# Local attention with in-place exponentials, PSUM operands, a new slot order and f16 three-product projections

## The chip, the cores and the metric

The program runs on one core of one Trainium2 chip. The metric is the device time of one execution in microseconds; the number quoted for a version is the median of several executions.

## What is computed

The input is 8 sequences of 512 tokens with 128 features. First comes a clustered attention with its own MLP, then two layers of rotary local attention, each followed by a gated FFN. The change touches only the local attention of the two layers:

```python
h = shift_token(x)
qkv = h @ wqkv                       # 128 -> 3*512
q = l2norm(q) * qs ; k = l2norm(k) * ksc
q, k = rotary_xpos(q, k)             # q*cos*scale + rotate_half(q)*sin*scale
sim = jnp.einsum('bhwid,bhwjd->bhwij', bq, bk)      # 8 heads of 64, window 64, own + previous window
attn = jax.nn.softmax(sim, axis=-1)                 # banded mask
out = jnp.einsum('bhwij,bhwjd->bhwid', attn, bv)
x = x + o @ wo
h = shift_token(x)                   # and its mean and variance, for the FFN
```

## The kernel before, in words

`local_attention` is called once per layer. The 8 x 512 tokens make 32 tiles of 128 tokens, four tiles to a sequence. Each of the five engines runs its own hand-written list of steps, one `slot(n)` per tile; semaphores alone tie the engines together. A tile passes through five slots: in slot n TensorE (PE) projects tile T = n to q, k and v; N = n-1 gets its norms; R = n-2 is transposed; U = n-3 gets scores, maxima and exponentials; O = n-4 gets its division by the row sums, the transposition of the probabilities and the product with v. At the end of a sequence, three more steps follow, a slot apart: the product with `wo` and the addition to x (slots with n mod 4 = 0), the token shift and its mean (0 and 1), the squares and their mean (1 and 2).

The steps that the change touches, with their lines before:

- PE: `project` (L1313) writes f32 products into a ring of two PSUM banks, used in turn with `transpose` (L1325) of the rotated q and k. `ring_free` says whose reader must be done before a bank is written again. `scores` (L1336 the mask, L1343 the products) writes `s_ps`, two PSUM banks. `prob_turn` (L1355) transposes the probabilities, `weigh` (L1369) multiplies them with v, L1399 is the product with `wo`.
- ScalarE (ACT): `take_raw` (L1556) copies q and k from the ring to SBUF as `raw`; `squares` (L1600); `take_qT` (L1563), `take_values` (L1579), `take_out` (L1571) copy from PSUM; `exps` (L1544) reads `s_ps`, writes `prob` in SBUF, head by head, with the row sum as accumulator; `inverse_norms` (L1588, L1591); `shift_tokens` (L1538, L1539) makes `hT`.
- VectorE (DVE): `share` (L1475, L1477) divides `prob` in SBUF by the sums; `maxima` is a reduction over `s_ps` (L1461) and a tiny product of two SBUF operands, the exponentials' bias (L1467); `rotate` (L1442) multiplies the swapped halves of `raw` by the sines, both operands in SBUF; `take_probT` (L1495) and `take_kT` (L1488) copy from PSUM; `norms` (L1451, and L1455 the clip).
- GpSimd (POOL): `polish` (L1644 to L1650, four tiny steps), `scale_keys` (L1670), `shift` (L1681, L1683), `spin` (L1657 the cosine product, L1663 the sum with `swapped`).

## Time and profile before

| | |
|---|---|
| runs shown | 1634.2, 1635.84, 1637.27 us; median 1635.84 |
| profiled execution | 1636.19 us, of which the span from first to last instruction is 1634.4 |
| busy over the whole span | PE 80%, DVE 78%, ACT 61%, POOL 53% |
| local attention, layer 0 and 1 | 358.2 and 360.6 us |
| gated FFN, layer 0 and 1 | 79.5 and 80.1 us |
| mean granted TensorE clock | 0.925 of full speed |

Busy time is the union of an engine's instructions. Times in the trace are microseconds from the start of the span. An f32 matmul of 512 columns stands as two instructions in the trace, an f16 one as one. An instruction's duration is a little longer than the distance to the next one's start, as the engines overlap the end of one with the start of the next.

### The profile page before, as it was taken

Reading aid. Unit: us, or ns where it says so; the run is one execution under the profiler, and the core shown is the slowest. Engines: PE = TensorE matmul, PEld = TensorE weight load, DVE = VectorE, ACT = ScalarE, POOL = GpSimd, SP = SyncE. Lnnn points to the kernel's source line nnn. Section 1 sums busy time; section 2 is a strip of 40 time slices with the busy share of each in tenths; the row PEclk is TensorE's granted clock in tenths of the full one; section 3 lists DMA queues with packets and bytes.
Section 4 is the critical chain, followed back from the end, with each engine's and each line's share of the span. In section 5 each row is a group of like instructions: output and inputs, shape, how many; then the busy total and the mean of one; then the engine's idle time right before and its main releaser. Section 6 shows DMA issues by size and latency. Waiting matters only on the chain. (4 is left out here: it accounts for less than half of the span.)

```text
span 1634.4 us, 26635 instructions
## 1 busy us (share of the span) xinstructions
PE 1314.9 (80%) x9094; PEld 619.7 (38%) x9156; DVE 1267.1 (78%) x1905; ACT 989.5 (61%) x2252; POOL 871.0 (53%) x989
## 2 busy tenths in 40 slices
PE   3488998989989875776788888868778888888596
PEld 1122222222222213453455555543335555555343
DVE  5778888878888634336999999959569999999593
ACT  4246666666666662225788887743257777777522
POOL 4566767676766001114777777730067777777100
PEclk8579999999999997787999999998979999999898
DMA  3433333333333101001111111101011111111001
GB/s 102 93 59 65 66 65 66 65 65 62 69 59 70 23 1 51 1 2 33 24 24 24 24 24 24 24 7 40 12 24 24 24 24 24 24 24 24 1 0 54
DMA packets 161402, 60.92 MB, mean 37 GB/s; under 512 B 139722, under 2 KB 153076, under 8 KB 161268
## 3 DMA queue, kind: packets, MB, share of 16 engines
q1 hardware_dynamic: 161268, 59.22, 17.1%
q8 instruction: 74, 1.21, 0.3%
q14 instruction: 60, 0.49, 0.1%
HBM read 8.73 MB, written 2.10 MB: 7 GB/s over the span
## 5 line engine op out<-in xcount | busy, mean ns | idle before, releaser
L639 DVE TENSOR_REDUCE row_max<-max_ps 128x2 f32<-128x1024 f32 x256 | 313.0, 1223 | 70.3 <-PE max_ps L451 68.9
L691 ACT ACTIVATE prob<-scores_ps 128x1024 f32<-128x1024 f32 x256 | 262.2, 1024 | 147.5 <-PE scores_ps L431 144.0
L1313 PE MATMUL la_ring<-lw_wqkv,la_hT 128*128 128x512 f32 x384 | 230.4, 687 | 26.5 <-ACT la_hT L1539 13.6
L1544 ACT ACTIVATE la_prob<-la_s,la_bias,la_inv 128x128 f32<-128x128 f32 x512 | 229.1, 474 | 32.0 <-DVE la_bias L1467 31.7
L1657 POOL TENSOR_TENSOR la_turned<-la_raw,lw_rot 128x1024 f32<-128x1024 f32 x64 | 168.5, 2632 | 128.9 <-ACT la_raw L1556 127.9
L431 PE MATMUL scores_ps<-stack 128*128 128x512 f16 x512 | 155.5, 386 | 41.9 <-ACT prob L691 41.1
L1663 POOL TENSOR_TENSOR la_turned<-la_turned,la_swapped 128x1024 f32<-128x1024 f32 x64 | 151.0, 2359 | 60.5 <-DVE la_swapped L1442 60.4
L1442 DVE TENSOR_TENSOR la_swapped<-la_raw,lw_rot 128x512 f32<-128x512 f32 x128 | 164.1, 1321 | 14.5 <-ACT la_raw L1556 14.5
L465 PE MATMUL heads_ps<-prob,v_pad 128*32 128x512 f32 x1024 | 137.3, 608 | 1.1 <-ACT prob L691 1.1
L1369 PE MATMUL la_o<-la_probT,la_v_back 128*64 128x64 f32 x1024 | 72.3, 239 | 69.6 <-DVE la_probT L1495 69.4
L451 PE MATMUL max_ps<-stack 24*128 24x512 f16 x512 | 102.5, 397 | 31.3 <-DVE row_max L639 18.9
L431 PEld LDWEIGHTS scores_ps<-stack 128*128 128x128 f16 x512 | 34.2, 97 | 208.7 <-ACT prob L691 161.4
L1544 ACT ACTIVATION_READ_ACCUMULATOR la_prob<-la_s,la_bias,la_inv 128x1 f32 x512 | 113.2, 221 | 0.0
L797 POOL TENSOR_TENSOR cl<-cl,cl_inv 128x512 f32<-128x512 f32 x60 | 63.0, 1049 | 85.1 <-DVE cl_inv L580 85.1
L1461 DVE TENSOR_REDUCE la_neg_max<-la_s 128x8 f32<-128x1024 f32 x64 | 78.3, 1223 | 33.7 <-PE la_s L1343 33.7
L1556 ACT ACTIVATE la_raw<-la_ring 128x512 f32<-128x512 f32 x128 | 77.2, 603 | 43.3 <-PE la_ring L1313 42.9
L1003 POOL TENSOR_TENSOR mlp_base<-X,Z 128x512 f32<-128x512 f32 x8 | 10.3, 1283 | 164.7 <-POOLq L885 93.0
L1369 PEld LDWEIGHTS la_o<-la_probT,la_v_back 128*64 128x64 f32 x1024 | 57.6, 144 | 100.3 <-issue 99.9
L1477 DVE TENSOR_TENSOR la_prob<-la_prob,la_inv_sum 128x512 f32<-128x512 f32 x128 | 89.2, 697 | 4.4
L1325 PEld LDWEIGHTS la_ring<-mlp_ident,la_turned 128*128 128x128 f32 x512 | 64.0, 142 | 66.9 <-issue 56.9
L1313 PEld LDWEIGHTS la_ring<-lw_wqkv,la_hT 128*128 128x128 f32 x384 | 62.7, 204 | 60.0 <-issue 28.9
L1814 ACT ACTIVATE ff_gate<-ff_g,lw_b 128x512 f32<-128x512 f32 (+1 forms) x48 | 32.9, 686 | 86.5 <-PE ff_g L1829 86.5
(164 smaller groups left out, 2894.9 us busy)
## 6 DMA issues: line engine op xcount, KB each, us to landing
la_v_back<-la_v_own SPq DMA_DIRECT2D x112, 128.0 KB, 2.3
X<-in_x SPq DMA_DIRECT2D x8, 256.0 KB, 5.3
stack<-stack_tok SPq DMA_TRANSPOSE x128, 3.2
out<-X SPq DMA_DIRECT2D x8, 256.0 KB, 2.4
lw_wqkv<-in_wqkv SPq DMA_DIRECT2D x2, 768.0 KB, 4.7
stack<-shift_row SPq DMA_DIRECT2D x64, 2.0 KB
lw_rot<-in_rot SPq DMA_DIRECT2D x2, 512.0 KB, 6.3
lw_w<-in_fw SPq DMA_DIRECT2D x2, 341.0 KB
```

The source lines that it names most:

```text
L431: mm = nc.tensor.matmul(scores_ps[:, i, :], stack[:, par, 1, h, kt * P:(kt + 1) * P], stack[:, par, 0, h, :], start=True, stop=True)
L451: mm = nc.tensor.matmul(max_ps[:, e, :], stack[rows, b % 2, 0, 2 * pair + e, qt * P:(qt + 1) * P], stack[rows, b % 2, 1, 2 * pair + e, :], ...
L465: mm = nc.tensor.matmul(heads_ps[32 * j:32 * j + 32, :], v_pad[:, par, kt, 4 * g + j, :], prob[:, c % 4, j, :], start=(kt == 0), stop=(kt ...
L639: nc.vector.tensor_reduce(row_max[:, grp % 2, w // 2, :, w % 2], max_ps[:], AX.X, ALU.max).then_inc(max_made, 1)
L691: nc.scalar.activation(prob[:, c % 4, 2 * pr:2 * pr + 2, :], scores_ps[:], ACT.Exp, scale=1.0 / LOGIT_SCALE).then_inc(exp_made, 1)
L1313: mm = nc.tensor.matmul(ring_ps[:, r % 2, :], hT[:, b % 2, t * P:(t + 1) * P], wqkv[:, at:at + INNER], start=True, stop=True)
L1369: mm = nc.tensor.matmul(o_ps[64 * e:64 * e + 64, pair, 64 * w:64 * w + 64], (v_back, v_own)[w][:, at, h, :], probT[:, h, 64 * w:64 * w + 6 ...
L1442: ins = nc.vector.tensor_tensor(dst[:, :, :, w, :], src[:, :, :, 1 - w, :], sines, ALU.mult)
L1477: nc.vector.tensor_tensor(prob[:, par, heads], prob[:, par, heads], inv_sum[:, heads].unsqueeze(2).to_broadcast([P, 4, KEYS]), ALU.mult).t ...
L1544: ins = nc.scalar.activation(prob[:, T % 2, h, :], s_ps[:, place(h), :], ACT.Exp, bias=bias[:, T % 2, h:h + 1], scale=inv[:, T % 4, h:h + ...
L1657: nc.gpsimd.tensor_tensor(spun, raw[:, T % 2].rearrange("p s (h f) -> p s h f", f=LD), rot[:, T % TPB, :, 0, :].unsqueeze(2).to_broadcast( ...
L1663: nc.gpsimd.tensor_tensor(turned[:, T % 2], turned[:, T % 2], swapped[:], ALU.add).then_inc(added_rot, 1)
```

## The change

The exponentials are written back over the scores in PSUM, and `share` takes them from there; `scores` of the next tile therefore waits for both halves of `share` and not for the exponentials. The halves are now the even and the odd heads, which lie in separate banks. `rotate` reads the ring in PSUM instead of `raw`, one side at a time, and so frees the ring bank. The projections use f16 high and low parts of tokens and weights (weights times 64), in three products with one accumulation; the parts of the weights are made once per layer, those of the tokens once per sequence (`round_tokens` on ACT, `split` on DVE). `take_out` moves from ACT to DVE, half of `take_probT` from DVE to ACT (`take_low`), `shift` from POOL to ACT. The order within a slot changes on all four engines.

```diff
-        PROJ_Q, TURN_Q, PROJ_K, TURN_K, PROJ_V = range(5)
+        PROJ_Q, PROJ_K, TURN_Q, PROJ_V, TURN_K = range(5)
...
                 if use in (PROJ_Q, PROJ_K):
-                    pe.wait_ge(raw_made, 2 * T + SIDE[use] + 1)
+                    pe.wait_ge(swap_made, 2 * T + SIDE[use] + 1)
...
-                mm = nc.tensor.matmul(ring_ps[:, r % 2, :], hT[:, b % 2, t * P:(t + 1) * P],
-                                      wqkv[:, at:at + INNER], start=True, stop=True)
+                for n, (hp, wp) in enumerate(((0, 0), (0, 1), (1, 0))):
+                    mm = nc.tensor.matmul(ring_ps[:, r % 2, :], h16[:, b % 2, hp, t * P:(t + 1) * P],
+                                          w16[:, wp, at:at + INNER], start=(n == 0), stop=(n == 2))
...
                 if T > 0:
-                    pe.wait_ge(exp_made, T)
+                    pe.wait_ge(shared, 2 * T)
...
+            nc.vector.scalar_tensor_tensor(out=w16[:, 1, 0:INNER], in0=wqkv[:, 0:INNER], scalar=W_SCALE,
+                                           in1=w16[:, 0, 0:INNER], op0=ALU.mult, op1=ALU.subtract
+                                           ).then_inc(w_low_q, 1)
+            def split(b):
+                dve.wait_ge(h_high, 2 * (b + 1))
+                x = batch_at(XT, b)
+                nc.vector.tensor_tensor(h16[0:64, b % 2, 1, :], x[0:64, :], h16[0:64, b % 2, 0, :],
+                                        ALU.subtract).then_inc(h_made, 1)
+                nc.vector.tensor_tensor(h16[64:P, b % 2, 1, 1:S], x[64:P, 0:S - 1], h16[64:P, b % 2, 0, 1:S],
+                                        ALU.subtract).then_inc(h_made, 1)
...
-                    sines = rot[:, t, :, 1, w * 32:(w + 1) * 32].unsqueeze(2).to_broadcast([P, 2, LH, 32])
-                    ins = nc.vector.tensor_tensor(dst[:, :, :, w, :], src[:, :, :, 1 - w, :], sines, ALU.mult)
+                    sines = rot[:, t, side, 1, w * 32:(w + 1) * 32].unsqueeze(1).to_broadcast([P, LH, 32])
+                    ins = nc.vector.scalar_tensor_tensor(out=dst[:, :, w, :], in0=src[:, :, 1 - w, :],
+                                                         scalar=1.0 / W_SCALE, in1=sines, op0=ALU.mult,
+                                                         op1=ALU.mult)
...
-                nc.vector.tensor_tensor(prob[:, par, heads], prob[:, par, heads],
+                nc.vector.tensor_tensor(prob[:, T % 2, heads], s_ps[:, heads],
...
-                    ins = nc.scalar.activation(prob[:, T % 2, h, :], s_ps[:, place(h), :], ACT.Exp,
+                    ins = nc.scalar.activation(s_ps[:, place(h), :], s_ps[:, place(h), :], ACT.Exp,
...
+            for side in (1, 2):
+                at = side * INNER
+                pool.wait_ge(w_high, side + 1)
+                nc.gpsimd.tensor_scalar(wqkv[:, at:at + INNER], wqkv[:, at:at + INNER], W_SCALE, None,
+                                        ALU.mult).then_inc(w_scaled, 1)
+                pool.wait_ge(w_scaled, side)
+                nc.gpsimd.tensor_tensor(w16[:, 1, at:at + INNER], wqkv[:, at:at + INNER],
+                                        w16[:, 0, at:at + INNER], ALU.subtract).then_inc(w_low_kv, 1)
...
             def slot(n):
                 T, N = tile_or_none(n), tile_or_none(n - 1)
+                if T is not None:
+                    spin(T)
                 if N is not None:
                     polish(N)
                     scale_keys(N)
-                if ended(n - 5) is not None:
-                    shift(ended(n - 5))
-                if T is not None:
-                    spin(T)
```

The order on VectorE, in a slot at the end of a sequence (n mod 4 = 0) and the start of the next one. Before:

```order
L1475 RECIPROCAL la_inv_sum<-la_sums 128x4
L1477 TENSOR_TENSOR la_prob<-la_prob,la_inv_sum 128x512
L1475 RECIPROCAL la_inv_sum<-la_sums 128x4
L1477 TENSOR_TENSOR la_prob<-la_prob,la_inv_sum 128x512
L1461 TENSOR_REDUCE la_neg_max<-la_s 128x8
L1467 TENSOR_TENSOR la_bias<-la_neg_max,la_inv 128x8
L1442 TENSOR_TENSOR la_swapped<-la_raw,lw_rot 128x16x32 x2
L1495 COPY la_probT<-la_pT 128x512 x2
L1451 TENSOR_REDUCE la_sumsq<-la_squares 128x16
L1455 SCALAR_TENSOR_TENSOR la_sumsq<-la_sumsq,la_minus_half 128x16
L1488 COPY la_kT<-la_ring 128x4x128
L1518 TENSOR_TENSOR XT<-la_m,XT 128x512
```

The same engine and place in the changed kernel:

```order
L1507 RECIPROCAL la_inv_sum<-la_sums 128x4
L1511 TENSOR_TENSOR la_prob<-la_s,la_inv_sum 128x512
L1526 COPY la_oT<-la_o 128x4x128
L1472 SCALAR_TENSOR_TENSOR la_swapped<-la_ring,lw_rot 128x8x32 x4
L1493 TENSOR_REDUCE la_neg_max<-la_s 128x8
L1499 TENSOR_TENSOR la_bias<-la_neg_max,la_inv 128x8
L1519 COPY la_probT<-la_pT 128x512
L1535 COPY la_kT<-la_ring 128x4x128
L1483 TENSOR_REDUCE la_sumsq<-la_squares 128x16
L1487 SCALAR_TENSOR_TENSOR la_sumsq<-la_sumsq,la_minus_half 128x16
L1568 TENSOR_TENSOR XT<-la_m,XT 128x512
```

The copy of the output and the rotation (four short operations) moved ahead of the maxima, which the exponentials wait for; one copy of `probT` is gone, and the other stands behind the bias.

The order on ScalarE, one slot of the middle of a sequence, before:

```order
L1579 ACTIVATE la_v_own<-la_ring 128x512
L1600 ACTIVATE la_squares<-la_raw 128x1024
L1556 ACTIVATE la_raw<-la_ring 128x512
L1563 ACTIVATE la_qT<-la_ring 128x512
L1544 ACTIVATE la_prob,la_sums<-la_s,la_bias,la_inv 128x128 x4
L1556 ACTIVATE la_raw<-la_ring 128x512
L1544 ACTIVATE la_prob,la_sums<-la_s,la_bias,la_inv 128x128 x4
L1588 ACTIVATE la_lnsq<-la_sumsq 128x16
L1591 ACTIVATE la_inv<-la_lnsq,la_half_ln 128x16
L1571 ACTIVATE la_oT<-la_o 128x4x128
```

And in the changed kernel:

```order
L1603 ACTIVATE la_raw<-la_ring 128x512 x2
L1659 ACTIVATE la_squares<-la_raw 128x1024
L1610 ACTIVATE la_probT<-la_pT 128x512
L1617 ACTIVATE la_qT<-la_ring 128x512
L1635 ACTIVATE la_v_own<-la_ring 128x512
L1592 ACTIVATE la_s,la_sums<-la_s,la_bias,la_inv 128x128 x8
L1644 ACTIVATE la_lnsq<-la_sumsq 128x16
L1647 ACTIVATE la_inv<-la_lnsq,la_half_ln 128x16
```

The copy of v moved ahead of the exponentials, and no copy of the ring stands between the exponentials any more.

The order on TensorE, a middle slot of the changed kernel up to the product with v (before, the two projections of q and k stood apart, v's stood last, and all eight transpositions of the probabilities stood together behind the scores):

```order
L1324 MATMUL la_ring<-lw_w,la_h 128x512 x6
L1365 MATMUL la_pT<-mlp_ident,la_prob 128x128 x4
L1347 MATMUL la_s<-lw_band,lw_identb 128x512 x2
L1354 MATMUL la_s<-la_kT,la_qT 64x128 x16
L1336 MATMUL la_ring<-mlp_ident,la_turned 128x128 x4
L1365 MATMUL la_pT<-mlp_ident,la_prob 128x128 x4
L1324 MATMUL la_ring<-lw_w,la_h 128x512 x3
L1336 MATMUL la_ring<-mlp_ident,la_turned 128x128 x4
```

The projection of v now stands between the scores and the last transposition of the slot, `la_ring<-...la_turned` for the keys.

## Rows read from the trace of the kernel before

**Rows 1.** Windows: first of four slots, and the four's sum: us, engines' busy time, clock.

```profile
840.43:850.90 10.47, 8.82 (x93) 5.51 (x93) 10.17 (x15) 8.93 (x27) 7.28 (x8) 1.00 0.11 26
...
sum 40.65, PE 34.34 PEld 21.30 DVE 39.25 ACT 32.63 POOL 31.89; mean PE 8.58 PEld 5.33 DVE 9.81 ACT 8.16 POOL 7.97
```

**Rows 2.** Timeline of VectorE, 919 to 964: start, us, instruction.

```profile
921.71 1.22 DVE L1461 TENSOR_REDUCE la_neg_max<-la_s 128x8 f32<-128x1024 f32 x1
922.96 2.07 DVE L1467 TENSOR_TENSOR la_bias<-la_neg_max,la_inv 128x8 f32<-128x8 f32 x1
924.96 1.28 DVE L1442 TENSOR_TENSOR la_swapped<-la_raw,lw_rot 128x512 f32<-128x512 f32 x2
926.16 1.28 DVE L1495 COPY la_probT<-la_pT 128x512 f32<-128x512 f32 x2
...
942.45 0.17 DVE L1467 TENSOR_TENSOR la_bias<-la_neg_max,la_inv 128x8 f32<-128x8 f32 x1
942.55 3.46 DVE L1442 TENSOR_TENSOR la_swapped<-la_raw,lw_rot 128x512 f32<-128x512 f32 x2
...
961.75 0.69 DVE L1477 TENSOR_TENSOR la_prob<-la_prob,la_inv_sum 128x512 f32<-128x512 f32 x1
962.36 1.22 DVE L1461 TENSOR_REDUCE la_neg_max<-la_s 128x8 f32<-128x1024 f32 x1
```

**Rows 3.** Timeline of GpSimd, 921 to 950.

```profile
922.66 2.35 POOL L1657 TENSOR_TENSOR la_turned<-la_raw,lw_rot 128x1024 f32<-128x1024 f32 x1
...
942.56 2.90 POOL L1657 TENSOR_TENSOR la_turned<-la_raw,lw_rot 128x1024 f32<-128x1024 f32 x1
946.15 2.35 POOL L1663 TENSOR_TENSOR la_turned<-la_turned,la_swapped 128x1024 f32<-128x1024 f32 x1 [0.69 <-DVE la_swapped L1442]
949.21 0.22 POOL L1644 TENSOR_TENSOR la_newton<-la_inv 128x16 f32<-128x16 f32 x1 [0.70 <-ACT la_inv L1591]
949.50 0.22 POOL L1646 TENSOR_TENSOR la_newton<-la_newton,la_sumsq 128x16 f32<-128x16 f32 x1
```

**Rows 4.** Groups by line, 760 to 1060: busy us, mean ns, idle before.

```profile
L1442 DVE TENSOR_TENSOR la_swapped<-la_raw,lw_rot 128x512 f32<-128x512 f32 x60 | 79.5, 1363 | 1.6 <-ACT la_raw L1556 1.6
L1467 DVE TENSOR_TENSOR la_bias<-la_neg_max,la_inv 128x8 f32<-128x8 f32 x29 | 26.5, 914 | 1.0
```

**Rows 5.** One operand in PSUM: one line's durations (min/median/max), VectorE's timeline.

```profile
L571 DVE TENSOR_TENSOR cl<-bench,cl_max x64: 680/681/693, 25.6 to 521.1; 128x512 f32<-128x512 f32 x64
...
1121.15 1.31 DVE L1773 SCALAR_TENSOR_TENSOR ff_prod<-ff_a,lw_b,ff_gate 128x512 f32<-128x512 f32 x2
```

**Rows 6.** Timeline of TensorE, 303 to 304 and 899 to 908.

```profile
303.46 0.61 PE L431 MATMUL scores_ps<-stack 128*128 128x512 f16 x2
304.00 0.39 PE L509 MATMUL bench<-ident,shift_tok 128*4 128x128 f16 x4
...
899.07 0.38 PE L1336 MATMUL la_s<-lw_band,lw_identb 128*128 128x512 bf16 x1 [0.46 <-issue]
900.41 1.12 PE L1313 MATMUL la_ring<-lw_wqkv,la_hT 128*128 128x512 f32 x2
...
903.55 0.60 PE L1325 MATMUL la_ring<-mlp_ident,la_turned 128*128 128x128 f32 x4
903.99 3.60 PE L1399 MATMUL la_m<-la_oT,lw_wo 128*128 128x512 f32 x8
```

**Rows 7.** Timeline of ScalarE, start of layer 0, and 928 to 934.

```profile
746.33 0.62 ACT L1539 ACTIVATE la_hT<-XT 64x511 f32<-64x511 f32 x1
...
928.61 0.48 ACT L1544 ACTIVATE la_prob<-la_s,la_bias,la_inv 128x128 f32<-128x128 f32 x1
928.96 0.23 ACT L1544 ACTIVATION_READ_ACCUMULATOR la_prob<-la_s,la_bias,la_inv 128x1 f32 x1
929.05 0.63 ACT L1619 ACTIVATE VAR<-la_m 128x512 f32<-128x512 f32 x1
...
932.20 0.60 ACT L1556 ACTIVATE la_raw<-la_ring 128x512 f32<-128x512 f32 x1 [0.16 <-PE la_ring L1313]
```

More of the change, by code:

```diff
@@ L749, in slot @@
                 if s["max"] is not None and s["max"] % UNITS == UNITS - 1:
-                    shift_tokens(s["max"] // UNITS)
+                    round_tokens(s["max"] // UNITS)
             over_slots(slot)
@@ L1130 @@
 QK_SCALE = 8.0
+W_SCALE = 64.0
 NEG = -1e30
@@ L1363, in weigh @@
                         pe.wait_ge(oT_made, T)
-                pe.wait_ge(pT_made, 2 * T + half + 1)
+                if half == 0:
+                    pe.wait_ge(pT_low, T + 1)
+                    pe.wait_ge(pT_high, T + 1)
                 for pair in (2 * half, 2 * half + 1):
@@ L1370, in weigh @@
                                                   (v_back, v_own)[w][:, at, h, :],
-                                                  probT[:, h, 64 * w:64 * w + 64], start=True, stop=True)
+                                                  probT[:, place(h), 64 * w:64 * w + 64], start=True, stop=True)
                 mm.then_inc(o_filled, 1)
@@ L1382, in slot @@
                 if O is not None:
-                    prob_turn(O)
+                    prob_turn(O, 1)
                 if T is not None:
-                    project(T, PROJ_K)
+                    project(T, PROJ_V)
+                if R is not None:
+                    transpose(R, TURN_K)
                 b = ended(n - 7)
@@ L1390, in slot @@
                                      ).then_inc(m_filled, 1)
-                if R is not None:
-                    transpose(R, TURN_K)
+                b = ended(n - 6)
+                if b is not None:
+                    pe.wait_ge(sh_made, 2 * (b + 1))
+                    nc.tensor.matmul(m_ps[:], mean_of[:], shifted[:], start=True, stop=True
+                                     ).then_inc(m_filled, 1)
                 b = ended(n - 5)
@@ L1401, in slot @@
                     mm.then_inc(m_filled, 1)
-                b = ended(n - 6)
-                if b is not None:
-                    pe.wait_ge(sh_made, 2 * (b + 1))
-                    nc.tensor.matmul(m_ps[:], mean_of[:], shifted[:], start=True, stop=True
-                                     ).then_inc(m_filled, 1)
                 if O is not None:
@@ L1409, in slot @@
                     weigh(O, 1)
-                if T is not None:
-                    project(T, PROJ_V)
             run(pe, slot)
@@ L1489, in take_kT @@
                                       ring_ps[:, r % 2, :].rearrange("p (c q) -> p c q", q=P)).then_inc(kT_made, 1)
[L1491 to L1496 removed]
             def slot(n):
[L1499 removed]
+                T, N, R, U, O, out = (tile_or_none(n - x) for x in (0, 1, 2, 3, 4, 5))
                 if O is not None:
@@ L1502, in slot @@
                     share(O, 1)
+                if out is not None:
+                    take_out(out)
+                if T is not None:
+                    rotate(T, 0)
+                    rotate(T, 1)
                 if U is not None:
                     maxima(U)
-                if N is not None:
-                    rotate(N)
+                if n % TPB == TPB - 1 and n + 1 < NT:
+                    split((n + 1) // TPB)
                 if O is not None:
-                    take_probT(O, 0)
-                    take_probT(O, 1)
+                    take_high(O)
+                if R is not None:
+                    take_kT(R)
                 if N is not None:
                     norms(N)
-                if R is not None:
-                    take_kT(R)
-                b = ended(n - 5)
-                if b is not None:
-                    x = batch_at(XT, b)
-                    dve.wait_ge(m_filled, m_count(b, W0))
-                    nc.vector.tensor_tensor(x, m_ps[:], x, ALU.add).then_inc(x_added, 1)
                 b = ended(n - 6)
@@ L1524, in slot @@
                                             ALU.subtract).then_inc(c_made, 1)
+                b = ended(n - 5)
+                if b is not None:
+                    x = batch_at(XT, b)
+                    dve.wait_ge(m_filled, m_count(b, W0))
+                    nc.vector.tensor_tensor(x, m_ps[:], x, ALU.add).then_inc(x_added, 1)
             run(dve, slot)
@@ L1531, in _, with round_tokens @@
             act.wait_ge(ready, 1)
-            def shift_tokens(b):
+            def round_tokens(b):
                 if b >= 2:
@@ L1595, in slot @@
                 T, N, R, U, O = (tile_or_none(n - x) for x in (0, 1, 2, 3, 4))
+                if T is not None:
+                    take_raw(T, 0)
+                    take_raw(T, 1)
                 if N is not None:
@@ L1627, in slot @@
                     nc.scalar.activation(csq[:], batch_at(C, b), ACT.Square).then_inc(csq_made, 1)
-                if O is not None:
-                    take_out(O)
-                if T is not None:
-                    take_values(T)
+                if N is not None:
+                    inverse_norms(N)
+                b = ended(n - 5)
+                if b is not None:
+                    shift(b)
+                b = ended(n - 7)
+                if b is not None:
+                    act.wait_ge(m_filled, m_count(b, SQUARE))
+                    nc.scalar.activation(batch_at(VAR, b), m_ps[:], ACT.Copy).then_inc(var_made, 1)
             run(act, slot)
```

160 lines of the change are left out of this document (85 added, 75 removed).

## The prediction

> **What bounds the kernel now.** I read the table of busy times first. Local attention takes 358.2 and 360.6 us of the 1634.4, twice 32 tiles; nothing outside it changes. Then the four slots of one sequence as windows [rows 1]: 40.65 us, 10.16 a tile, with VectorE busy for 39.25 of it, TensorE for 34.34, ScalarE for 32.63, GpSimd for 31.89, TensorE at full granted clock. VectorE bounds the stage. Its timeline says with what [rows 2, 3]: the bias, a product of 128x8, takes 0.17 us at 942.45 and 2.07 us at 922.96; the long one ends at 925.03, just when GpSimd's L1657, begun at 922.66, ends (925.01). The two rotations take 1.28 us together at 924.96, beside no large GpSimd operation, and 3.46 at 942.55; there GpSimd's L1657 takes 2.90 where 2.35 is its free time, so each waited for the other. Both VectorE operations have two operands in SBUF. Over 300 us the rotations have a mean of 1363 ns and the bias 914 [rows 4]: per tile 2 x (1.36 - 0.64) + (0.91 - 0.17) = 2.2 us of VectorE's 9.8 is waiting for GpSimd.
>
> **What the change removes.** An operation of VectorE with one operand in PSUM does not show this: L571 ran 64 times with 680 to 693 ns [rows 5], in a stage where GpSimd works all the time. Rotation and division now have their data operand in PSUM, so I expect no such wait in either. The bias, the clip (L1487) and `split` keep two SBUF operands.
>
> VectorE per tile then, by distances from start to start: two divisions 0.83 each (some 0.2 for the reciprocal, 0.61 from 961.75 to the next start), copy of the output 0.60, four rotations, maxima 1.25, bias 0.10, two copies 1.20, norms 1.3 (a reduction of 1024 elements, like the maxima) [rows 2]. For a rotation of 256 elements the nearest row is L1773, two of 512 in 1.31 [rows 5], 0.62 apart as the tail overlaps; half the elements at 0.96 per ns less is 0.35, and 0.62 would be the bound if nothing shrank. I take 0.35: 1.4 for four. Sum 7.6, plus 1.2 for the two batch additions and some 1.3 for `split` in four tiles: 8.2 a tile. ScalarE keeps its 32.63 in four tiles, one kind of copy for another, and gets `shift`, two copies of 0.62: 33.9, 8.5 a tile. TensorE loses: an f32 projection keeps it 0.86 (two parts of 0.43), three f16 products take 0.65 at 0.22 (0.27 by the nearest pair, 303.46 to 304.00, which gives 0.81 [rows 6]). GpSimd has 31.89, waiting for VectorE included, and loses `shift`: under 7.8. No engine's own work is above 8.5, so the chain of waits decides.
>
> **The chain of a slot.** Clock zero is the end of the exponentials of the tile before. `share` of the second half ends at 0.94. Only now may TensorE write the scores; mask and scores keep it 1.34 (899.07 to 900.41 [rows 6]), begun 0.32 after the release, so until 2.6, readable at 2.75. VectorE meanwhile: output copy to 1.5, rotations to 2.9 (raw, two copies of 0.60 on ScalarE behind the logarithm and the seed, is there at 0.9 and 1.4 [rows 7]), maxima to 4.15, bias to 4.25. TensorE: transposition of q to 3.04 (0.44 for four), of the second probabilities to 3.5, v's projection to 4.13, readable at 4.35 to 4.5, transposition of k to 4.7. ScalarE takes v at 4.4 and only then, at 4.9, begins the exponentials: the last starts 3.07 later and its sum ends 0.58 after that (928.61, 928.96 + 0.23 [rows 7]). A plain slot is 4.9 + 3.65 = **8.55 us**. VectorE's rest (copies, norms, first `share`) ends at 8.1, hidden by the exponentials by only 0.45; without that cover it is the next addend.
>
> Extras in four slots. (a) `wo`, eight instructions 0.43 apart [rows 6], 3.5 us, stands before `weigh`: it ends at 8.2, and VectorE's addition to x (0.68) waits for it ahead of the next `share`: both halves then end at 10.5 and not 9.4, +1.1. (b) `shift` on ScalarE waits for x, then 1.28, and `round_tokens` 1.28 stands before v in the same slot; half of it lies in ScalarE's gaps: +0.4. (c) `split` is two SBUF operations of 0.6 behind the bias. GpSimd asks for L1720 at 4.8, between the two; if it gets in, the second waits 2.35: then `take_high`, norms and `share` are late by 2.7, otherwise by 0.5. Taken: 1.6. Queued behind it are `take_high` (for it `weigh`, and the next projections) and the clip (for it ScalarE's logarithm). (d) The moved `shift` frees GpSimd of 1.2 in four, which had waits of its own: nothing. Group of four: 4 x 8.55 + 1.1 + 0.4 + 1.6 = 37.3 against 40.65, 0.83 a tile. I count 28 of 32 tiles at this difference: 23.2 us a layer.
>
> Against it, at each layer's start the parts of the weights: ScalarE makes three copies of about 0.6 behind the rounding (746.33 [rows 7]), then VectorE a low part (0.7) and two `split` operations (1.3): the first projection is 2.5 later, and those of k and v wait for GpSimd's pairs. I take 3 us (2 to 4). Net 20.2 a layer, 40.5 in all: 1636.2 - 40.5 = 1595.7, **1596 us**; the profiled execution's 1636.19 is 0.35 above the median of the runs shown, which is nothing here.
>
> ScalarE's store to PSUM in place of SBUF has no row; the nearest is the exponential to SBUF at 0.44 apart [rows 7]. I bound it by 0.05 either way, 0.4 on the chain of a slot, 22 us in all, and take zero.
>
> A row and a rule of the Trainium skill differ on the price of PSUM. The rows have a VectorE operation of 512 elements from PSUM to SBUF beginning 0.60 before the next (maxima to copies, two in 1.28 [rows 2]), the same as from SBUF. "VectorE: DVE Perf Modes", in its section on the TRN2 errata, gives 120 fixed cycles with a PSUM source against 58 from SBUF. By the page two divisions and four rotations would cost 0.06 more each, at most 0.3 of a slot on the chain, and the time would be about 1612; the measured rows are nearer to this case, and no term goes by the page.
>
> **Rivals.**
> 1. *The bias falls into the cosine product (slower).* The bias is asked for at 4.15, GpSimd's L1720 starts when k's transposition is done, 4.8. If the rotations cost 0.52 each and not 0.35, or the maxima come 0.7 later, the bias waits until 7.15, the exponentials start at 7.2, the slot is 10.9, and since all offsets start anew from `share`, each following slot repeats it. Group 44.5, 28 tiles worse by 0.96, 3 at the start: 1636 + 60 = 1696. For it: 2.07 us at 922.96 is this very wait [rows 2]. Against: the margin of 0.65. It decides from about 1.2 slots of four: 2.35 x 1.2 eats the gain of 3.35 less the start.
> 2. *The same wait in one slot of four*, or 2 us of other waits (a late `raw` behind `shift`, `weigh` behind `split`): group 39.65; 4 us a layer: 1628. For it: today's bias waits are of just this kind, 0.17 to 2.07.
> 3. *`split` gets through in one piece and f16 products hide*: group 36.0 or less, 9.0 a tile, 1575 down to 1560.
> 4. *No net change*: VectorE waits for GpSimd with a PSUM operand too, so that the rotations still pay 1.4 a tile: about 1636, 1632 to 1640, or slightly slower with the start. L571 speaks against it.
>
> **How the numbers follow.** The forecast with its own ends (`split` 0.5 or 2.7, f16 0.22 or 0.27, rotations, start): 1575 to 1618, chance 0.54. Rival 2, 1618 to 1632: 0.18. Rival 3, below 1575: 0.06. Rival 4 within 0.2% 0.04, slightly slower 0.04. Rival 1: 0.14. Range 1564 to 1650: leaves out most of rival 1 and the tail of 3. Changes below 0.2%, 3 us, can't be told from none. Faster 0.78, same 0.04, slower 0.18.
>
> **What the profile after would show.** Rotations near 0.4 us with no long ones; divisions at 0.69; maxima 8.5 apart in plain slots, 37 in four; ScalarE's wait before the exponentials ended by itself (v) rather than by VectorE's bias; GpSimd's L1720 released by TensorE's transposition of k. The granted clock stays near full in the stage, as TensorE still works for some 6.9 of 8.55. Wrong if the bias (L1499) has a mean near 2, if the exponentials are further apart than 0.44, or if the plain slot is bounded by something that I hold to be covered: VectorE's rest, with 0.45 to spare, is the first.

## The result and the profile after

The changed kernel takes 1627.6 us (median of 14 runs, 1618.38 to 1632.43) against 1635.99 us before (14 runs, 1631.52 to 1638.87): ratio 0.9946, 95% interval 0.9929 to 0.9963. It is faster, by 8 us and not by the forecast 40. The profiled execution took 1627.39 us with a span of 1625.6.

The busy times of the page, whole span:

```profile
PE 1270.7 (78%) x9284; PEld 606.9 (37%) x9348; DVE 1218.6 (75%) x2067; ACT 1011.8 (62%) x2290; POOL 802.6 (49%) x965
```

Windows from one maxima to the next, four slots in the middle of layer 0, the answer to [rows 1] (us, then busy time of PE, PEld, DVE, ACT, POOL, granted clock, DMA share, GB/s):

```profile
839.32:847.83 8.51, 7.50 (x93) 4.79 (x94) 7.95 (x17) 7.99 (x27) 6.43 (x8) 1.00 0.14 33
847.83:859.70 11.87, 7.73 (x91) 5.29 (x92) 10.71 (x18) 8.19 (x26) 7.72 (x8) 0.90 0.05 11
859.70:870.18 10.48, 10.43 (x99) 6.63 (x101) 8.69 (x16) 8.74 (x26) 6.58 (x7) 0.95 0.12 27
870.18:879.59 9.41, 7.56 (x94) 4.86 (x96) 8.58 (x16) 9.01 (x28) 6.09 (x7) 1.00 0.13 31
sum 40.27, PE 33.21 PEld 21.57 DVE 35.92 ACT 33.93 POOL 26.82; mean PE 8.30 PEld 5.39 DVE 8.98 ACT 8.48 POOL 6.71
```

The rows are the plain slot, the slot with `split`, the one with the product with `wo` and the addition to x, and the one with the rounding. The plain slot is where the forecast had it (8.51, forecast 8.55). The group of four is not: 40.27 against 37.3 forecast and 40.65 before. The three extras were priced at 1.6, 1.1 and 0.4 and came to 3.36, 1.97 and 0.90 in this group; over the twelve steady groups of both layers (all but the first and the last of each) their means are 2.97, 1.86 and 0.83, and the group's is 39.78. The granted clock is 0.90 and 0.95 in two slots, 1.00 in the other two.

VectorE in the slot with `split`, where [rows 2] had two products and two rotations:

```profile
847.83 1.22 DVE L1493 TENSOR_REDUCE la_neg_max<-la_s 128x8 f32<-128x1024 f32 x1
849.08 0.17 DVE L1499 TENSOR_TENSOR la_bias<-la_neg_max,la_inv 128x8 f32<-128x8 f32 x1
849.17 0.68 DVE L1455 TENSOR_TENSOR la_h<-XT,la_h 64x512 f16<-64x512 f32 x1
849.88 0.69 DVE L1457 TENSOR_TENSOR la_h<-XT,la_h 64x511 f16<-64x511 f32 x1
...
851.91 1.22 DVE L1483 TENSOR_REDUCE la_sumsq<-la_squares 128x16 f32<-128x1024 f32 x1
853.17 2.06 DVE L1487 SCALAR_TENSOR_TENSOR la_sumsq<-la_sumsq,la_minus_half 128x16 f32<-128x16 f32 x1
855.15 0.17 DVE L1507 RECIPROCAL la_inv_sum<-la_sums 128x4 f32<-128x4 f32 x1
...
859.70 1.22 DVE L1493 TENSOR_REDUCE la_neg_max<-la_s 128x8 f32<-128x1024 f32 x1 [0.93 <-PE la_s L1354]
```

GpSimd beside it:

```profile
850.01 2.77 POOL L1720 TENSOR_TENSOR la_turned<-la_raw,lw_rot 128x1024 f32<-128x1024 f32 x1 [1.49 <-PE la_ring L1336]
852.86 2.34 POOL L1726 TENSOR_TENSOR la_turned<-la_turned,la_swapped 128x1024 f32<-128x1024 f32 x1
```

Both `split` operations take here what they take with nothing in their way; it is GpSimd's product, begun at 850.01 inside the second, that takes 2.77 and not 2.35. The victim is the next VectorE operation with two SBUF operands, the clip of 128x16: asked for 0.3 us after GpSimd's sum had begun, it takes 2.06 and ends as the sum ends (855.20). Behind it stand the two divisions and ScalarE's logarithm.

So it went in eleven of the twelve steady slots with `split`. In one, in layer 1, the order was the other one. GpSimd's product began at 1326.56, just ahead of the second `split` operation:

```profile
1326.65 2.80 DVE L1457 TENSOR_TENSOR la_h<-XT,la_h 64x511 f16<-64x511 f32 x1
1332.05 0.17 DVE L1487 SCALAR_TENSOR_TENSOR la_sumsq<-la_sumsq,la_minus_half 128x16 f32<-128x16 f32 x1
```

There `split` waits and the clip is free, and the slot takes 11.07 at a granted clock of 1.00, where the other order at that clock gives 10.86. So one wait of about 2 us is paid in either case. TensorE in the slot at 847.83, which had the usual order:

```profile
851.43 0.34 PE L1381 MATMUL la_o<-la_probT,la_v_back 128*64 128x64 f32 x4 [1.57 <-DVE la_probT L1519]
...
852.52 1.47 PE L1324 MATMUL la_ring<-lw_w,la_h 128*128 128x512 f16 x6
856.10 0.66 PE L1365 MATMUL la_pT<-mlp_ident,la_prob 128*128 128x128 f32 x4 [2.11 <-DVE la_prob L1511]
857.21 0.50 PE L1347 MATMUL la_s<-lw_band,lw_identb 128*128 128x512 bf16 x1 [0.46 <-DVE la_prob L1511]
857.65 1.99 PE L1354 MATMUL la_s<-la_kT,la_qT 64*64 64x128 f32 x32
859.56 1.11 PE L1336 MATMUL la_ring<-mlp_ident,la_turned 128*128 128x128 f32 x4
```

TensorE had sat idle for 1.57 us before the weighing, and sat idle for 2.11 and 0.46 for the divisions, and the 32 products of the scores then took 1.99 us where other slots have 1.10: the granted clock stood at its lower level, 1.2 GHz.

Groups of VectorE, 760 to 1060, the answer to [rows 4]:

```profile
L1472 DVE SCALAR_TENSOR_TENSOR la_swapped<-la_ring,lw_rot 128x256 f32<-128x256 f32 x120 | 42.3, 414 | 4.5 <-POOL la_turned L1726 3.4 <-ACT la_raw L1603 1.1
L1487 DVE SCALAR_TENSOR_TENSOR la_sumsq<-la_sumsq,la_minus_half 128x16 f32<-128x16 f32 x31 | 29.3, 944 | 1.1
L1499 DVE TENSOR_TENSOR la_bias<-la_neg_max,la_inv 128x8 f32<-128x8 f32 x30 | 5.0, 166 | 1.0
```

The rotations fell from 79.5 us to 42.3, the bias from 26.5 to 5.0. The clip rose from 7.0 us (mean 242 ns before) to 29.3: the clip now waits for much of what the bias waited for. It takes 2.06 us in those eleven slots and about 0.65 in most others (median of all 0.645 us); the latter costs the plain slot nothing, as the run without the clip shows below.

**The whole balance**, from the starts of the maxima in both layers, before and after: the first four distances of each layer 79.1 and 71.6 (-7.5); the next 24 of each, 491.2 and 477.4 (-13.8); the last three 55.0 and 54.8 (-0.2); from the stage's start to the first maxima 52.3 and 60.7 (+8.4); from the last maxima to the stage's end 41.1 and 46.7 (+5.6). Together -7.5 us. I had forecast -46.5 for the slots, +6 for the starts and nothing for the ends. Of the 33 us that are missing, 25 are in the slots.

The ends hold a thing of their own. Windows of the changed kernel, 1084 to 1091.55, the weighing and the last product with `wo`:

```profile
1084.00:1086.30 2.30, 1.53 (x29) 1.34 (x26) 0.69 (x1) 0.00 (x0) 0.00 (x0) 0.50 0.02 7
1086.31:1091.55 5.24, 5.24 (x8) 2.08 (x8) 0.00 (x0) 0.00 (x0) 0.00 (x0) 0.70 0.00 0
```

And of the kernel before, the same work:

```profile
1087.30:1090.12 2.82, 2.03 (x37) 1.54 (x37) 1.23 (x2) 0.60 (x1) 0.00 (x0) 1.00 0.00 0
1090.12:1093.82 3.70, 3.70 (x8) 1.43 (x8) 0.00 (x0) 0.00 (x0) 0.00 (x0) 1.00 0.00 0
```

The eight instructions take 5.24 where they took 3.70, at a granted clock of 0.70 instead of 1.00. Layer 1 ends in the same way, with 5.24 for 3.70.

### The profile page after: what moved, and what is told of

The parts are those of the page before. It is cut to its first block and busy times, and to the rows that moved or that the text cites. A ratio compares the mean times of both kernels' runs of the same rounds, so it can differ in the third digit from the quotient of the medians.

```text
span 1625.6 us, 27387 instructions
## 1 busy us (share of the span) xinstructions
PE 1270.7 (78%) x9284; PEld 606.9 (37%) x9348; DVE 1218.6 (75%) x2067; ACT 1011.8 (62%) x2290; POOL 802.6 (49%) x965
## 5 line engine op out<-in xcount | busy, mean ns | idle before, releaser
L1592 ACT ACTIVATE la_s<-la_s,la_bias,la_inv 128x128 f32<-128x128 f32 x512 | 223.0, 442 | 7.6 <-DVE la_bias L1499 7.1
L1720 POOL TENSOR_TENSOR la_turned<-la_raw,lw_rot 128x1024 f32<-128x1024 f32 x64 | 155.4, 2428 | 139.1 <-PE la_ring L1336 137.6
L431 PE MATMUL scores_ps<-stack 128*128 128x512 f16 x512 | 155.3, 385 | 41.9 <-ACT prob L691 41.1
L1324 PE MATMUL la_ring<-lw_w,la_h 128*128 128x512 f16 x576 | 155.1, 399 | 32.0 <-DVE la_h L1457 21.2
L1365 PE MATMUL la_pT<-mlp_ident,la_prob 128*128 128x128 f32 x512 | 82.5, 285 | 49.8 <-DVE la_prob L1511 49.1
L1592 ACT ACTIVATION_READ_ACCUMULATOR la_s<-la_s,la_bias,la_inv 128x1 f32 x512 | 111.1, 217 | 0.0
L1472 DVE SCALAR_TENSOR_TENSOR la_swapped<-la_ring,lw_rot 128x256 f32<-128x256 f32 x256 | 90.6, 414 | 25.5 <-POOL la_turned L1726 13.7
L1336 PE MATMUL la_ring<-mlp_ident,la_turned 128*128 128x128 f32 x512 | 86.1, 294 | 7.8 <-DVE la_swapped L1472 6.8
L1511 DVE TENSOR_TENSOR la_prob<-la_s,la_inv_sum 128x512 f32<-128x512 f32 x128 | 88.4, 691 | 4.4
L1381 PE MATMUL la_o<-la_probT,la_v_back 128*64 128x64 f32 x1024 | 67.7, 230 | 26.2 <-DVE la_probT L1519 25.5
L1365 PEld LDWEIGHTS la_pT<-mlp_ident,la_prob 128*128 128x128 f32 x512 | 59.9, 145 | 75.7 <-DVE la_prob L1511 73.1
L1324 PEld LDWEIGHTS la_ring<-lw_w,la_h 128*128 128x128 f16 x576 | 52.2, 101 | 87.6 <-issue 27.5
```

What stands on the lines that cost most here:

```text
L431: mm = nc.tensor.matmul(scores_ps[:, i, :], stack[:, par, 1, h, kt * P:(kt + 1) * P], stack[:, par, 0, h, :], start=True, stop=True)
L1324: mm = nc.tensor.matmul(ring_ps[:, r % 2, :], h16[:, b % 2, hp, t * P:(t + 1) * P], w16[:, wp, at:at + INNER], start=(n == 0), stop=(n == 2))
L1365: mm = nc.tensor.transpose(pT_ps[:, j, :], prob[:, T % 2, j, :], ident[:])
L1472: ins = nc.vector.scalar_tensor_tensor(out=dst[:, :, w, :], in0=src[:, :, 1 - w, :], scalar=1.0 / W_SCALE, in1=sines, op0=ALU.mult, op1=AL ...
L1511: nc.vector.tensor_tensor(prob[:, T % 2, heads], s_ps[:, heads], inv_sum[:, heads].unsqueeze(2).to_broadcast([P, 4, KEYS]), ALU.mult).then ...
L1592: ins = nc.scalar.activation(s_ps[:, place(h), :], s_ps[:, place(h), :], ACT.Exp, bias=bias[:, T % 2, h:h + 1], scale=inv[:, T % 4, h:h + ...
```

## The experiments

**Take `split` out of VectorE's way, in three ways.** First, f32 projections as before, so no `split` and no parts of the weights; the rest of the change stays.

```diff
-                for n, (hp, wp) in enumerate(((0, 0), (0, 1), (1, 0))):
-                    mm = nc.tensor.matmul(ring_ps[:, r % 2, :], h16[:, b % 2, hp, ...], w16[:, wp, at:at + INNER], ...)
+                mm = nc.tensor.matmul(ring_ps[:, r % 2, :], hT[:, b % 2, ...], wqkv[:, at:at + INNER], start=True, stop=True)
...
-                    split((n + 1) // TPB)
```

> The changed kernel with the projections of before: f32 tokens and weights in one product, no weight parts, no split of the tokens; all else of the change stays. Theory A (what the change lost against my 37.3 us for four slots lies in the slot with split: two VectorE operations of 0.7, the clip that then waits 2.06 behind GpSimd's sum, TensorE's idle gap, and half clock for the scores): the split slot falls from 11.9 to about 9, a plain slot rises from 8.5 to 8.7, four slots take 37.5 to 38, the start of each layer is 3.5 shorter; about 1592 us (1585 to 1600). Theory B (the extras come from the product with wo and ScalarE's late shift, and split only fills time that is lost anyway): four slots stay near 39.5, only the start is gained; 1615 to 1622.

Measured 1602.95 us, ratio 0.9798 (0.9782 to 0.9814). The slots (plain, `split`, `wo`, rounding) are 8.72, 8.74, 10.65, 9.41: the slot that had `split` costs nothing extra. The time is 3 us above the upper end of Theory A, whose slots came true and whose start did not: the first maxima come 32.1 and 32.6 us behind the stage's start in the two layers, against 30.0 and 30.8 in the changed kernel. Without the parts of the weights the start is no shorter.

Second, the two subtractions of `split` go to GpSimd, one slot after the other, each behind `scale_keys`.

```diff
-                if n % TPB == TPB - 1 and n + 1 < NT:
-                    split((n + 1) // TPB)
...
+                if n % TPB == 1 and n + 3 < NT:
...
+                    nc.gpsimd.tensor_tensor(h16[0:64, b % 2, 1, :], x[0:64, :], h16[0:64, b % 2, 0, :],
...
+                if n % TPB == 2 and n + 2 < NT:
...
+                    nc.gpsimd.tensor_tensor(h16[64:P, b % 2, 1, 1:S], x[64:P, 0:S - 1], h16[64:P, b % 2, 0, 1:S],
```

> The changed kernel with the two split operations of each sequence on GpSimd, in its idle time at the end of the slots with n mod 4 = 1 and 2; the f16 products and the weight parts stay. Theory A: the split slot falls to about 8.6 to 9.2, four slots take about 37.3, the start is unchanged: about 1590 us (1583 to 1600). Theory B: 1615 to 1625. If GpSimd's two operations push its cosine product over the bias, slots of 10.9 appear and it gets slower than 1627.

Measured 1592.16 us, ratio 0.9726 (0.9699 to 0.9754); slots 8.51, 8.53, 9.93, 9.41, clock 1.00 in each, in ten of the twelve steady groups. In the other two the clock is lower in two slots (10.15 and 9.38 at 0.91 in one group, 10.06 and 10.81 at 0.84 and 0.92 in the other).

Third, `split` stays on VectorE and the clip goes. This kernel leaves out the lower bound on the sum of squares (its factor -1/2 moves into the logarithm and the Newton step).

```diff
-                nc.vector.scalar_tensor_tensor(out=sumsq[:, par], in0=sumsq[:, par], scalar=1e-24,
-                                               in1=minus_half[:], op0=ALU.max, op1=ALU.mult)
```

> The changed kernel without the clip (the maximum with 1e-24 is left out; the factor -0.5 moves into a GpSimd step that is there anyway), so that VectorE has no operation with two SBUF operands between the maxima and the next division, except the bias and split. Theory A: in the split slot the 2 us behind GpSimd's sum fall away and VectorE's own 1.4 stays; the slot falls by 1.5 to 2, the others by 0 to 0.2, and TensorE's clock stays full behind it: 1600 to 1608 us. Rival (the 1.4 us of split alone, ahead of the copy of probT, make the slot long; the clip's wait is covered): 1619 to 1627.

Measured 1584.67 us, ratio 0.9681 (0.9659 to 0.9703), a larger gain than the 1600 to 1608 of Theory A: the slot lost 3.06 us where I had expected 1.5 to 2. Its windows, in the order `split`, `wo`, rounding, plain:

```profile
880.81:889.62 8.81, 6.99 (x93) 4.62 (x93) 8.62 (x17) 8.08 (x26) 6.84 (x8) 1.00 0.06 15
889.62:899.50 9.88, 9.88 (x100) 6.02 (x100) 7.97 (x17) 8.75 (x26) 7.38 (x8) 1.00 0.13 29
899.50:908.90 9.40, 7.76 (x95) 4.85 (x95) 8.01 (x15) 9.00 (x28) 6.09 (x7) 1.00 0.13 30
908.90:917.41 8.51, 7.49 (x94) 4.88 (x94) 7.39 (x15) 7.99 (x27) 6.41 (x8) 1.00 0.14 33
sum 36.60, PE 32.12 PEld 20.36 DVE 31.98 ACT 33.82 POOL 26.72; mean PE 8.03 PEld 5.09 DVE 8.00 ACT 8.46 POOL 6.68
```

`split` itself, still there, costs the slot 0.30. So the 3.36 of the changed kernel needs both: `split` moves the clip back behind the start of GpSimd's sum, and the clip then waits for it. Either one taken away frees the slot, and its clock is then 1.00 in all twelve steady groups without the clip and in eleven with `split` on GpSimd. Both at once bring nothing more:

> No clip and split on GpSimd together, on the changed kernel. If the waits between VectorE and GpSimd are all the excess, the split slot is 8.5 as any plain slot, four slots take 36.3: 1581 to 1587 us, hardly less than e3_no_clip, which had 8.82 for that slot. If GpSimd, now with two operations more, becomes what is waited for, it is slower than e3_no_clip (1585).

Measured 1586.9 us, ratio 0.9695 (0.9679 to 0.9712), slots 8.51, 8.53, 9.93, 9.41.

**What the lower clock costs.** 18 transpositions of the identity into a bank that is overwritten just after fill TensorE's idle time in the `split` slot.

```diff
+                    if O % TPB == 0 and O > 0:
+                        pe.wait_ge(pT_low, O)
+                        for k in range(18):
+                            nc.tensor.transpose(pT_ps[:, k % 4, :], ident[:], ident[:])
```

> The changed kernel with 18 more transpositions of the identity on TensorE, ahead of the first transposition of probabilities in the slots with n mod 4 = 0, into a PSUM bank half that is overwritten just after; they fill the gap of 2.1 us in which TensorE waits for the late division. Theory A2 (the clip's wait of 2 us costs a slot more than 2 us because TensorE stands idle, and its granted clock then falls to half for the scores): the granted clock stays at 1.00, the scores take 1.10 and not 1.99, the slot with split falls from 11.9 to about 10.9, 1612 to 1618 us. Rival (the slot's extra is all wait, the clock's fall is covered): 1624 to 1632, since 2 us of work are added.

Measured 1613.38 us, ratio 0.9863 (0.9842 to 0.9883). TensorE's timeline of this kernel:

```profile
852.72 2.13 PE L1395 MATMUL la_pT<-mlp_ident 128*128 128x128 f32 x18
855.01 0.66 PE L1365 MATMUL la_pT<-mlp_ident,la_prob 128*128 128x128 f32 x4 [0.16 <-DVE la_prob L1515]
855.91 0.59 PE L1347 MATMUL la_s<-lw_band,lw_identb 128*128 128x512 bf16 x2 [0.24 <-DVE la_prob L1515]
856.43 1.10 PE L1354 MATMUL la_s<-la_kT,la_qT 64*64 64x128 f32 x32
```

The scores are back at 1.10, the slots 10.87, 9.93, 9.41, 8.50. The clip still waits 2.07. So in the group shown, 1.0 us in the `split` slot and 0.55 in the next is clock (on the mean of the twelve groups 0.61 and 0.44), and useless work in the gap gains 14 us over the changed kernel. It does not always help. In the group at 1309.72, where `split` again waits for GpSimd and TensorE's one idle piece is 3.90 us, the clock falls all the same, and the 18 transpositions come on top:

```profile
1309.72:1323.61 13.89, 9.99 (x109) 7.35 (x108) 10.96 (x18) 8.21 (x25) 7.42 (x8) 0.88 0.04 9
```

**Does the PSUM operand matter, and where?** The rotations read `raw` in SBUF again, and the ring bank is free behind ScalarE's copy; all else as changed.

```diff
-                src = ring_ps[:, r % 2, :]...
+                src = raw[:, T % 2, side]...
```

> The changed kernel with the rotation read from raw in SBUF again, still in four operations and at its new place; the ring bank is free after ScalarE's copy. Theory A (the operand in PSUM is what frees VectorE of GpSimd): the rotations stand where GpSimd does its polish steps and the scaling of the keys, each tile pays 0.5 to 1.5 us, 1655 to 1710 us. Rival (the new place in the slot alone avoids GpSimd): within 5 us of 1627.

Measured 1686.85 us, ratio 1.0303 (1.0271 to 1.0334). And the exponentials go to `prob` in SBUF again, divided there in place, with the scores waiting only for the exponentials:

```diff
-                    pe.wait_ge(shared, 2 * T)
+                    pe.wait_ge(exp_made, T)
...
-                nc.vector.tensor_tensor(prob[:, T % 2, heads], s_ps[:, heads],
+                nc.vector.tensor_tensor(prob[:, T % 2, heads], prob[:, T % 2, heads],
...
-                    ins = nc.scalar.activation(s_ps[:, place(h), :], s_ps[:, place(h), :], ACT.Exp,
+                    ins = nc.scalar.activation(prob[:, T % 2, place(h), :], s_ps[:, place(h), :], ACT.Exp,
```

> The changed kernel with one part undone: the exponentials are written to SBUF, the division runs in place in SBUF, and the scores wait for the exponentials, not for the division. Theory A (a VectorE operation with two SBUF operands waits for GpSimd, one with a PSUM operand doesn't): each division now has two SBUF operands and can meet a GpSimd operation of 2.35 us; the scores may start 0.9 us earlier, but the divisions' mean rises from 0.69 to over 1.0 and the maxima and the bias behind them come late: 1640 to 1700 us. Rival B (the long wait of the scores for the division is what keeps a plain slot at 8.5, and SBUF divisions meet GpSimd seldom): plain slots of 7.8 to 8.2, divisions with a mean below 0.75, 1600 to 1618.

Measured 1687.36 us, ratio 1.0315 (1.0296 to 1.0335). The group of rotations in the first kernel, and of divisions in the second:

```profile
L1472 DVE SCALAR_TENSOR_TENSOR la_swapped<-la_raw,lw_rot 128x256 f32<-128x256 f32 x115 | 62.7, 603 | 3.6 <-POOL la_turned L1727 2.5 <-ACT la_raw L1604 1.1
```

```profile
L1509 DVE TENSOR_TENSOR la_prob<-la_prob,la_inv_sum 128x512 f32<-128x512 f32 x53 | 67.8, 1280 | 1.8
```

The divisions' mean rises from 691 ns to 1280 in this window, the longest takes 2820. Undoing either PSUM operand costs 59 or 60 us, the waits that its edit moves and a lower mean clock (0.902 for 0.921) included, and makes the change a loss of 3%. In both kernels the operations that got two SBUF operands again show the long waits: the rotations' mean is 603 ns where it was 414.

**The other two extras.** On the kernel without the clip: half of the product with `wo` left out (so the outputs' second half doesn't reach x).

```diff
-                    for c in range(4):
+                    for c in range(2):
```

> e3_no_clip with half of the product with wo left out (two of four chunks, four instructions fewer, 1.7 us of TensorE in each slot with n mod 4 = 0). Theory C (the slot of the addition to x is long since TensorE's product ends late and the addition stands before the next division): its 9.88 falls to about 8.7 to 9.0, four slots 35.6: 1568 to 1575 us. Rival (it is VectorE's and ScalarE's added copies): no more than 3 us below 1585.

Measured 1587.12 us, ratio 0.9698 (0.9679 to 0.9717): no gain. The slot fell only from 9.88 to 9.31, though TensorE lost 1.75 us, and elsewhere the slots rose. Windows of this kernel, three slots in a row:

```profile
923.52:932.84 9.32, 8.78 (x100) 5.62 (x100) 7.97 (x17) 8.22 (x25) 7.39 (x8) 1.00 0.13 31
932.84:942.75 9.91, 8.08 (x92) 4.70 (x91) 8.00 (x16) 9.80 (x29) 6.57 (x7) 0.94 0.12 28
942.75:952.39 9.64, 8.62 (x94) 5.79 (x95) 7.48 (x14) 7.54 (x26) 5.92 (x8) 0.89 0.12 29
```

In the groups ahead the second and third of these took 9.43 and 8.51 or 8.50; here, at 0.94 and 0.89, 9.91 and 9.64. These two slots cost 1.6 us more than in a group at full clock. In the profiled executions that happens in six of the twelve steady groups here and in two of twelve in the kernel that this one started from, while the `wo` slots gained 0.57 each: the lower clock takes back most of it. Next, the rounding behind the exponentials:

```diff
-                if n % TPB == 1 and n + 3 < NT:
-                    round_tokens((n + 3) // TPB)
...
                     exps(U, 1).then_inc(exp_made, 1)
+                if n % TPB == 1 and n + 3 < NT:
+                    round_tokens((n + 3) // TPB)
```

> e3_no_clip with the rounding of the tokens (two copies of 0.63 on ScalarE) behind the exponentials instead of ahead of the copy of v, in the slots with n mod 4 = 1. Theory D (these 1.28 us lie on the chain, ahead of v and the exponentials, and make that slot 9.41 where a plain one has 8.51): the slot falls to 8.6 to 8.9, 1573 to 1578 us. Rival (the copies of x's shift ahead of raw make it long, the rounding lies in a gap): the slot stays at 9.41 or gets longer, 1583 to 1590.

Measured 1583.55 us, ratio 0.9674 (0.9657 to 0.9692), the same as without the move: the rounding slot rose to 9.86, the plain one fell to 8.15, and the sum of the two stayed. Then `shift` back on GpSimd as before the change, also without the clip:

```diff
-                nc.scalar.activation(shifted[0:64, :], x[0:64, :], ACT.Copy)
+                nc.gpsimd.tensor_copy(shifted[0:64, :], x[0:64, :])
```

> On the kernel without the clip: the shift goes back from ScalarE to GpSimd, as before the change. It tests two terms of my sum, the shift and rounding on ScalarE (I took 0.4 us in four slots, and measured 0.9) and the relief of GpSimd (I took nothing). Theory A: the 0.9 us of the slot behind the addition to x is ScalarE's, so without the shift this slot falls from 9.41 to below 9.0, and the group of four from 36.6 to about 36.1: 1573 to 1582. Rival B: GpSimd's two copies (1.2 us) delay its next product, and with it the bias or the transposition: group 36.6 or more, 1583 to 1610.

Measured 1589.79 us, ratio 0.9721 (0.9706 to 0.9735). The slot stays at 9.40, and in one group is 9.81 at a granted clock of 0.94: `shift` is not what it costs. The changed kernel's own trace says what does. In the last group of each layer there is no next sequence to round, and the slot takes 8.64 (8.63 in layer 1):

```profile
1031.40:1040.04 8.64, 7.52 (x93) 4.82 (x95) 8.45 (x17) 7.83 (x26) 6.00 (x7) 1.00 0.14 33
```

So 0.77 of the 0.90 is the rounding, with 1.18 us less of ScalarE, and wherever the rounding stands within these two slots it costs the same. Last, f32 projections without the clip (a form that also leaves out the bound):

> f32 projections (no split, no low parts, no copies of the weights) and no clip. It prices the f16 products by themselves, once neither kernel waits at split or clip. Without the clip the f16 version takes 1584.7. The f32 projections without it: 3 x 0.21 more of TensorE a tile, but 3.9 us less at each layer's start. If TensorE has room in every slot (Theory A): 1575 to 1583. If it has none in the slot with the product with wo (B): 1585 to 1600, that slot at 10.6.

Measured 1603.3 us, ratio 0.9806 (0.979 to 0.9822), slots 8.72, 8.74, 10.66, 9.40. That is case B, its slot as expected and its time 3 us above the range. The start is not 3.9 us shorter: the first maxima come 29.9 and 30.0 us behind the stage's start, against 29.9 and 30.7 in the f16 version without the clip. Its `wo` slot as a window:

```profile
852.70:863.36 10.66, 10.61 (x96) 6.26 (x98) 8.06 (x17) 8.96 (x27) 7.27 (x8) 1.00 0.11 27
```

TensorE is busy for 10.61 of 10.66, and in the f16 version for 9.88 of 9.88 (above): this slot is bounded by TensorE, and the f16 products shorten it by 0.78. Without the clip they are worth 1603.3 - 1584.7 = 19 us; in the changed kernel, where they bring `split`, they cost 1627.6 - 1602.95 = 25 us.

**The whole computation, mended.** The clip stays, `split` is on GpSimd, the rounding behind the exponentials (both edits above).

> The whole computation, with the low parts of the tokens made by GpSimd in two slots (as in the run with split on GpSimd) and the rounding behind the exponentials. If the rounding's place is free to choose (the run with the rounding late moved 0.45 us from one slot to the next and no more), the time is that of split on GpSimd, 1586 to 1595. If the rounding late costs where the low parts then come late (GpSimd waits for them within the same slot), a slot of the group rises above 9.9: over 1597.

Measured 1586.54 us, ratio 0.97 (0.9686 to 0.9715): slots 8.30, 8.52, 9.93, 9.85, and 41 us below the changed kernel.

## Why the prediction was wrong in its size

- **Rotations, divisions and bias: right.** With one operand in PSUM 256 rotations took 410 to 426 ns, none longer, at 0.33 from start to start (0.35 taken). Both experiments that put an operand back into SBUF show the wait again. Rival 4 fell. All 128 divisions took 0.69. My row for this, L571, was weaker than I said: 29 of its 64 runs overlap work of GpSimd, which is not "all the time"; none of them is longer. The bias has a mean of 166 ns: rival 1 did not come. The Trainium skill ("GPSIMD Engine Reference", section "1. Specifications") names the condition: contention with VectorE's instructions "with two SBUF inputs". The rows agree, and add that the wait does not shrink with the operation: the clip of 128x16 goes from 0.17 to 2.06, the `split` operation of 64x511 from 0.69 to 2.80.
- **The plain slot: right**, 8.55 against 8.51, mean of all such slots 8.59. That agrees with my chain (`share`, the scores, v's copy, the exponentials), and the store to PSUM by ScalarE shows no extra cost. Two of my sums were off without effect on it: VectorE's terms per tile add up to 7.5 and not 7.6, and TensorE is busy for 7.50 of the 8.51 and not for 6.9.
- **The failed step: extra (c), `split`, "Taken: 1.6".** The step asked only whether GpSimd gets in between the two `split` operations, and said of the clip that it stood behind them. In eleven of the twelve steady slots it doesn't get in: its product starts inside the second, and its sum starts 0.3 before the clip is asked for. The clip has two SBUF operands and I had listed it with the other two, but looked for its collision nowhere. Delaying VectorE's queue shifts every later operation with two SBUF operands against GpSimd's. So the branch that I had priced at 0.5 does not exist here: with GpSimd in between, `split` waits and the slot's extra is 2.56; without, the clip waits and it is 2.35, both at full clock. Of this 0.30 is `split` itself. Over the twelve steady groups the extra is 2.97 on average, 0.61 of it clock. Removing the clip, or moving `split` to GpSimd, brings 43 or 35 us.
- **"The granted clock stays near full": wrong, and unpriced.** I had looked at a mean (6.9 of 8.55 busy), while the idle time of the `split` slot sits in a few long pieces. After 2.11 us idle the scores ran at the 1.2 GHz level in the slot shown, and in eight of the twelve steady ones for at least a part. Filling the gap brought 1.0 and 0.55 us in two slots. At the stage's end, where TensorE also idles for divisions, the eight `wo` instructions took 5.24 for 3.70; I had priced the ends at nothing and they cost 2.8 each, 1.54 of it in these eight. When the level falls is not the same in each group, so the same work gives slots of 10.86 to 12.17:

```profile
899.39:910.50 11.11, 11.06 (x99) 6.96 (x101) 8.69 (x16) 8.74 (x26) 6.58 (x7) 0.90 0.11 26
910.50:920.71 10.21, 8.36 (x93) 5.50 (x95) 8.66 (x16) 9.56 (x28) 6.62 (x7) 0.91 0.12 27
920.71:930.03 9.32, 8.30 (x93) 5.60 (x95) 8.04 (x15) 7.47 (x25) 5.90 (x7) 0.92 0.13 30
```

  These three slots of the changed kernel, one group later than those shown first, take 11.11, 10.21 and 9.32 where others take 9.93, 9.41 and 8.51, with the clock at 0.90 to 0.92.
- **Extra (a), 1.1: mis-sized.** Its mechanism was wrong too: not the addition to x is last but TensorE, full for 9.88 of 9.88. Without the lower clock it is 1.37 to 1.42, with it 1.97 in the group shown and 1.86 on average. Leaving out 1.75 us of it gives 0.57; in that kernel the rotations then wait 0.74 for ScalarE's `raw`, which stands behind `shift`.
- **Extra (b), 0.4: mis-sized, 0.90.** ScalarE is busy for 9.00 of 9.40 there; the rounding does not lie in gaps, as I had said of half of it. Slots without rounding show 0.13 in place of 0.90. Moving it behind the exponentials keeps the sum of the two slots at 18.0 (17.9 before the move), and moving `shift` away does nothing.
- **Start: near in size, wrong in mechanism.** The start was +4.2 a layer for 3 taken, just beyond my 2 to 4, and I had put it down to the parts of the weights. They do delay the first rotation, to 8.7 us behind the stage's start from 6.2 in the kernels with f32 projections, the 2.5 that I took. But those kernels have their first maxima 29.9 to 32.6 behind the start, against 30.0 and 30.8 in the changed kernel; before the change it was 26.0 and 26.2. So at least most of the delay is in what all these kernels share, and no run tells which part of it. That my 3 came near is luck.
- **Count: partly right.** "28 of 32 tiles at this difference" assumed 10.16 to 9.33 a tile; the 24 steady ones gave 0.29 each. On the other side the first four slots, which I had left out, gained 3.8 a layer.
- **Which rival it was.** The time of rival 2 (1628), "2 us of other waits" in one slot of four, is the case that came, with the wait at the clip, where the rival had named `raw` and `weigh`, and the clock as its second half. Its group of 39.65 is near the 39.78 measured. That its time is right to the microsecond is luck: the ends (+5.6) and the first slots (-7.5), neither in its sum, nearly cancel. I gave it 0.18. The PSUM rule of the Trainium skill (1612 by it) does not bear: an operation of 512 elements from PSUM still starts 0.60 before the next, and the plain slot came out without its term.

What stays open: why the clock falls after the gap in some groups and keeps up in others with the same timeline, and what lengthens the stage's start.

## What to carry to other kernels

When an operation is put into VectorE's queue, list every later operation of that queue with two operands in SBUF, however tiny, and place each against GpSimd's long ones at its new time; the tiny ones at the head of a chain cost most. A PSUM operand takes an operation off that list. Look at TensorE's idle time as pieces, not as a share: with idle pieces of 1.57, 2.11 and 0.46 us in one slot the clock fell here in eight slots of eleven, and with the piece of 1.57 alone, without the clip, in none of twelve.
